# Attention's layer norm for samples 2 to 7 by sums and constant-tile products, in place of transposes both ways

## The reference, cut to what matters

```
def layernorm(x, gamma, beta):
    mu = jnp.mean(x, axis=-1, keepdims=True)
    var = jnp.var(x, axis=-1, keepdims=True)
    return (x - mu) * jax.lax.rsqrt(var + EPS) * gamma + beta
h = layernorm(x, gamma1, beta1)
Q = (h @ Wq + bq) ...
```

## Time and profile before

| what | value |
|---|---|
| median of 3 runs | 1611.33 us (1608.42 to 1615.32) |
| profiled execution, span from first to last instruction | 1610.9 us |
| granted TensorE clock, mean | 0.995 |
| PE busy | 1585.8 us, 98% |
| PEld / DVE / ACT / POOL busy | 1299.5 / 1166.6 / 982.8 / 410.9 us |
| HBM | 125 GB/s over the span |
| a load or store of a whole sample (1024 KB), issue to landing | 4.3 to 5.1 us, median |

### The profile page before, as it was taken

The page is one execution under the profiler, slowest core; times in us unless marked ns, Lnnn a source line. Parts: engine busy times, 40 slices in busy tenths (PEclk is TensorE's granted clock), DMA queues, the critical chain, the costliest instruction groups (busy, mean ns, idle before and its releaser), DMA issues.

```text
span 1610.9 us, 27177 instructions
## 1 busy us (share of the span) xinstructions
PE 1585.8 (98%) x9296; PEld 1299.5 (81%) x9298; DVE 1166.6 (72%) x2767; ACT 982.8 (61%) x2331; POOL 410.9 (26%) x605
## 2 busy tenths in 40 slices
PE   7999999999999999999999999999999999999999
PEld 4688786777777777777777688898999999999998
DVE  7999888786969686868778576785655656565643
ACT  6888766887878787878778755352433324242422
POOL 8998810313222313131312110201010110202010
PEclk8999999999999999999999999999999999999999
DMA  7042135543545444444337435866464555556361
GB/s 308 0 183 97 66 126 126 149 130 92 138 95 139 100 115 122 111 116 115 88 90 214 167 152 207 303 262 232 178 234 170 213 225 188 212 178 265 142 211 68
DMA packets 62257, 254.79 MB, mean 158 GB/s; under 512 B 10628, under 2 KB 16004, under 8 KB 46760
## 3 DMA queue, kind: packets, MB, share of 16 engines
q1 hardware_dynamic: 62120, 253.06, 48.2%
HBM read 153.93 MB, written 48.23 MB: 125 GB/s over the span
## 4 chain that ended last, share of the span: by engine, by line
PE 90%; POOL 3%; DMA 2%; DVE 2%; ACT 1%; issue 1%; SPq 1%; POOLq 0%; DVEq 0%; ACTq 0%
PE psum L83 24%; PE psum L84 23%; PE psum L85 23%; PE psum L1529 5%; PE psum L1549 5%; PE psum L1579 4%; PE psum L1470 1%; DMA k_weights<-w_factors 1%; PE psum L1478 1%; PE psum L2451 1%; DMA k_raw<-in_t_w 1%; POOL k_gs_square L252 1%; POOL k_gs_root L247 1%; ACT psum L1229 1%; POOL k_gs_scaled L256 1%
## 5 line engine op out<-in xcount | busy, mean ns | idle before, releaser
L1229 ACT ACTIVATE psum<-psum,b_mx 128x512 f32<-128x512 f32 (+3 forms) x512 | 258.9, 509 | 63.2 <-DVE b_mx L990 62.0
L990 DVE CUSTOM_DVE_ANT_0 psum<-psum,b_mask 128x512 f32<-128x512 f32 (+3 forms) x512 | 244.7, 506 | 53.0 <-PE psum L1529 48.1
L2398 ACT ACTIVATE k_act<-k_stack_f,k_smalls 128x512 f32<-128x512 f32 x112 | 80.9, 722 | 303.6 <-DVE k_stack_f L2237 297.1
L1241 ACT ACTIVATE k_exps<-psum 128x512 f32<-128x512 f32 (+1 forms) x384 | 194.6, 532 | 59.4 <-PE psum L1549 58.1
L864 POOL TENSOR_SCALAR_AFFINE_SELECT k_exps<-k_exps 128x256 f32<-128x256 f32 x256 | 96.4, 413 | 381.0 <-ACT k_exps L1241 379.1
L2097 POOL TENSOR_SCALAR k_result<-k_result,k_pb 128x512 f32<-128x512 f32 x32 | 59.2, 1866 | 434.9 <-DVE k_result L2156 434.9
L2216 DVE TENSOR_TENSOR k_act_lo<-k_act,k_act_hi 128x512 fp32r<-128x512 f32 x112 | 77.2, 690 | 120.6 <-ACT k_act_hi L2401 120.6
L83 PE MATMUL psum<-k_act_hi,k_w_hi 128*128 128x512 f32 x384 | 150.8, 393 | 0.0
L84 PE MATMUL psum<-k_act_lo,k_w_hi 128*128 128x512 f32 x384 | 150.5, 392 | 0.0
L85 PE MATMUL psum<-k_act_hi,k_w_lo 128*128 128x512 f32 x384 | 150.2, 391 | 0.0
L2237 DVE TENSOR_TENSOR k_raw<-psum,k_raw 128x256 f32<-128x256 f32 x168 | 70.5, 421 | 106.0 <-PE psum L85 95.4
(11 more groups left out here) (372 smaller groups left out, 4418.2 us busy)
## 6 DMA issues: line engine op xcount, KB each, us to landing
k_stack<-w_factors SPq DMA_DIRECT2D x35, 1792.0 KB, 7.7
k_stack<-k_samples SPq DMA_DIRECT2D x384, 128.0 KB, 2.4
k_weights<-w_factors SPq DMA_DIRECT2D x17, 1792.0 KB, 7.5
x<-k_tokens SPq DMA_DIRECT2D x10, 1024.0 KB, 4.3
k_tokens<-x SPq DMA_DIRECT2D x8, 1024.0 KB, 5.1
d<-k_result SPq DMA_DIRECT2D x32, 256.0 KB, 2.9
k_raw<-x SPq DMA_DIRECT2D x8, 1024.0 KB, 4.8
k_raw<-d SPq DMA_DIRECT2D x8, 1024.0 KB, 7.1
```

Of the source, the lines that this page charges most:

```text
L990: last = dve.tensor_tensor_reduce(got, got, mask[:, S - width:S], -INV_SQRT_DH, -2.0 * MASKED, ALU.add, ALU.min, mx[n % 2][:, h, t:t + 1])
L1229: act.activation(sc(n, u)[:, at:at + width], sc(n, u)[:, at:at + width], ACT.Exp, bias=mx[n % 2][:, h, t:t + 1], scale=-1.0, accum_out=sum ...
L1241: act.activation(exps[n % 2][:, h, at:at + width], by_key(n, u)[:, 0:width], ACT.Exp, scale=INV_SQRT_DH).then_inc(k_act, 1)
L2398: act.activation(act_f[:], whole_tile, ACT.Gelu, bias=small(smalls, "b1", 2 * pair % M + second)).then_inc(pair_gelu, 1)
```

## The change

For samples 2 to 7 nothing is turned. POOL adds the four pieces of a sample to one 128x512 tile, splits that sum in a high and a low part (`sample_sum`, five instructions), and PE multiplies both with a constant 128x128 tile of 1/512 (`mean_product`, two matmuls), which leaves the mean of each token on every partition. ACT copies it to SBUF (`mean_copy`), DVE subtracts it from the four pieces (`centre`), ACT squares them (`squares`), POOL sums and splits again (`square_sum`), PE multiplies again (`variance_product`), ACT makes a first reciprocal root by Ln and Exp on 128x512 (`rough_rstd`), DVE does one Newton step in three instructions (`refine`) and multiplies the four pieces (`multiply`), ACT applies gamma and beta from SBUF (`scale_spread`), POOL splits as before (`split_spread`). The 32 transposes, four copies, four scalings out of PSUM, four `statistics`, four `normalise` and one `prepare_rstd` of each such sample go. `BANK_ORDER` loses eight uses and gains two; `values_out(b, 3)` and `values_out(b, 2)` move by a place on DVE. On SP, the load `sample_in(b + 2)` goes from group 1 to the end of group 2. POOL makes two constants in the head. The rest of the diff renumbers semaphores that the samples 0, 1 and the second layer norm now share.

```diff
 (BANK_ORDER)
-     ("tin", 1, 0), ("q", 0, 2), ("k", 0, 2), ("tin", 1, 1), ("tin", 1, 2), ("tin", 1, 3), ("v", 0, 3),
+     ("mean", 1, 0), ("q", 0, 2), ("k", 0, 2), ("v", 0, 3), ("var", 1, 0),
      ("v", 0, 2)),
-    (("tb", 1, 0), ("q", 0, 3), ("k", 0, 3), ("tb", 1, 1), ("tb", 1, 2), ("wo", -1, 0), ("tb", 1, 3), ...
+    (("q", 0, 3), ("k", 0, 3), ("wo", -1, 0), ("wo", -1, 1), ("q", 1, 0), ("k", 1, 0), ...
 (SP, slots)
-                if g == 1 and b + 2 < B:
-                    sample_in(b + 2)
...
                 stack_rows(n + 1, (2, 3))
+                if g == 2 and b + 2 < B:
+                    sample_in(b + 2)
 (POOL)
+        def sample_sum(b):
+            wait_taken(pool, ("st", b, 1))
+            pool.tensor_tensor(tok[:, 0, :], x[:, 0, :], x[:, 1, :], ALU.add).then_inc(mean_sums, 1)
+            for j in (2, 3):
+                wait_taken(pool, ("st", b, j))
+                wait_sums(pool, b, j - 1)
+                pool.tensor_tensor(tok[:, 0, :], tok[:, 0, :], x[:, j, :], ALU.add).then_inc(mean_sums, 1)
+            wait_sums(pool, b, 3)
+            pool.tensor_copy(sums_r[:, 0, :], tok[:, 0, :]).then_inc(mean_sums, 1)
+            wait_sums(pool, b, 4)
+            pool.tensor_tensor(sums_r[:, 1, :], tok[:, 0, :], sums_r[:, 0, :].bitcast(F32), ALU.subtract)...
 (POOL, slots)
                 cut_later(n - 2, 1)
                 if g == 2 and b + 1 < B:
                     for j in range(J):
-                        split(b + 1, j)
+                        split_spread(b + 1, j)
+                if g == 1 and b + 1 < B:
+                    square_sum(b + 1)
                 cut_later(n - 1, 0)
-                if g == 1 and b + 1 < B:
-                    prepare_rstd(b + 1)
+                if g == 0 and b + 1 < B:
+                    sample_sum(b + 1)
 (DVE)
+        def centre(b, j):
+            wait_taken(dve, ("mean", b, 0))
+            dve.tensor_tensor(tok[:, j, :], x[:, j, :], tok[:, J - 1, :], ALU.subtract).then_inc(mean_out, 1)
+        def refine(b, part):
+            bank, y, step = pj(("var", b, 0)), x[:, 3, :], x[:, 0, :]
+            if part == 0:
+                wait_squares(dve, b, J + 2)
+                dve.scalar_tensor_tensor(step, bank, LN_EPS, y, ALU.add, ALU.mult).then_inc(pj_dve, 1)
+            (parts 1 and 2: step = (step * -0.5) * y; step = (step + 1.5) * y)
+        def multiply(b, j):
+            wait_spread(dve, b, J + 2)
+            dve.tensor_tensor(tok[:, j, :], tok[:, j, :], x[:, 0, :], ALU.mult).then_inc(mean_out, 1)
 (DVE, first_steps from max_unit(n + 1, 3) on)
+            max 3, max 4, centre 0, centre 1, max 5, maxima_out(n, 1), centre 2, centre 3, max 6, max 7, ...
+            ... values_out(b, 3), maxima_out(n + 1, 0), max 11, refine 0
 (DVE, last_steps)
+            max 0, values_out(b, 2), shift_rows(n - 1, 1), refine 1, max 1, refine 2, max 2, max 3, multiply 0,
+            max 4, maxima_out(n - 1, 1), multiply 1, max 5 to 7, qk_out, shift_rows, qk_out, multiply 2, max 8,
+            max 9, multiply 3, max 10
 (ACT, first_steps)
+            exps(n+1, 2), by_key(n-1, 11), mean_copy, by_key(n, 0), exps(n+1, 3), exps 4, by_key 1, exps 5,
+            squares 0, 1, 2, log_sums, exps 6, squares 3, exps 7, by_key 2 to 5, ctx_high, by_key 6, exps 8,
+            by_key 7, exps 9, by_key 8, by_key 9, rough_rstd, by_key 10, exps 10
 (ACT, last_steps)
+            exps(n, 0) to (n, 5), scale 0, by_key 0, by_key 1, exps 6, scale 1, by_key 2, log_sums, exps 7,
+            by_key 3, by_key 4, ctx_high, exps 8, scale 2, by_key 5, exps 9, scale 3, by_key 6, ...
 (PE)
+        def mean_product(b):
+            wait_sums(pe, b, 5)
+            out = claim(("mean", b, 0))
+            pe.matmul(out, mean_of[:], sums_r[:, 0, :], start=True, stop=False)
+            pe.matmul(out, mean_of[:], sums_r[:, 1, :], start=False, stop=True).then_inc(pj_full, 1)
 (mean_product stands after qk_piece(b, 2, 1); variance_product, built alike, after score_by_key(n, 9))
```

More of the change, by code:

```diff
@@ L596 @@
 AFTER = B
+SPREAD = range(2, B)
+TURNED_AT = {b: k for k, b in enumerate(b for b in range(B + 1) if b not in SPREAD)}
 U_TILES = ((T - 1,), (T - 2, 0), (1,))
@@ L795, in sample_in @@
             if b:
-                wait_full(sp, ("tin", b - 1, T - 1))
+                if b - 1 in SPREAD:
+                    wait_normalised(sp, b - 1)
+                else:
+                    wait_full(sp, ("tin", b - 1, T - 1))
                 sp.wait_ge(x2_st, 16 * b)
@@ L1116, in first_steps @@
                 max_unit(n + 1, k)
+            shift_rows(n, 1)
+            max_unit(n + 1, 3)
+            max_unit(n + 1, 4)
             if b + 1 < B:
-                statistics(b + 1, 0)
-            shift_rows(n, 1)
-            for k in range(3, 6):
-                max_unit(n + 1, k)
+                centre(b + 1, 0)
+                centre(b + 1, 1)
+            max_unit(n + 1, 5)
             maxima_out(n, 1)
+            if b + 1 < B:
+                centre(b + 1, 2)
+                centre(b + 1, 3)
             max_unit(n + 1, 6)
@@ L1156, in last_steps @@
             qk_out(n + 1, 1)
-            for k in range(8, 11):
-                max_unit(n, k)
+            multiply(b + 1, 2)
+            max_unit(n, 8)
+            max_unit(n, 9)
+            multiply(b + 1, 3)
+            max_unit(n, 10)
             ctx_low(n - 2)
@@ L1259, in scale_back, with mean_copy, squares, rough_rstd @@
                            scale=small(smalls, gamma, j)).then_inc(pj_act, 1)
+        def mean_copy(b):
+            wait_full(act, ("mean", b, 0))
+            act.activation(tok[:, J - 1, :], pj(("mean", b, 0)), ACT.Copy).then_inc(pj_act, 1)
+        def squares(b, j):
+            wait_spread(act, b, j + 1)
+            if j == 0:
+                act.wait_ge(x2_st, 16 * (b + 1))
+            act.activation(x[:, j, :], tok[:, j, :], ACT.Square).then_inc(mean_act, 1)
+        def rough_rstd(b):
+            y = x[:, 3, :]
+            wait_full(act, ("var", b, 0))
+            act.wait_ge(mask_made, 5)
+            wait_sums(act, b, 8)
+            act.activation(y, pj(("var", b, 0)), ACT.Ln, bias=eps[:]).then_inc(mean_act, 1)
+            wait_squares(act, b, J + 1)
+            act.activation(y, y, ACT.Exp, scale=-0.5).then_inc(mean_act, 1)
+        def scale_spread(b, j):
+            wait_normalised(act, b, j + 1)
+            act.activation(tok[:, j, :], tok[:, j, :], ACT.Identity, bias=small(smalls, "beta1", j),
+                           scale=small(smalls, "gamma1", j)).then_inc(mean_act, 1)
         def p_parts(b):
@@ L1354, in last_steps @@
             log_sums(n - 1, 1)
-            scale_back(b + 1, 0)
-            for k in range(6):
-                exponentials(n, k)
+            exponentials(n, 0)
+            exponentials(n, 1)
+            exponentials(n, 2)
+            exponentials(n, 3)
+            exponentials(n, 4)
+            exponentials(n, 5)
+            scale_spread(b + 1, 0)
             exponentials_by_key(n - 1, 0)
@@ L1682, in first_steps @@
             qk_piece(b, 2, 1)
+            if b + 1 < B:
+                mean_product(b + 1)
             score(n + 1, 2)
@@ L2463, in spread @@
         def spread(b):
-            pe.wait_ge(mv_set, T * b)
+            pe.wait_ge(mv_set, before + T * b)
             for t in range(T):
```

165 lines of the change are left out of this document (106 added, 59 removed).

## The result

The changed kernel took 1625.59 us (median of 4 runs, 1623.54 to 1629.66), the kernel before 1610.09 on the same chip (4 runs, 1608.42 to 1615.32). The ratio is 1.0100 with a 95% interval of 1.0085 to 1.0115: slower by one per cent. The forecast was 1614, with a range that ended at 1623. The profiled execution of the changed kernel has a span of 1627.9 us, the longest of its four (the others 1621.8, 1622.6, 1625.2).

The account below looks back on a forecast made before the run. PE, busy 98% of the span, was taken as the bound. Per sample, 2.52 us won against 3.2 of stalls, small gaps allowed for, lost 0.5; six samples gave +3.0, hence 1614 us, range 1598 to 1623.

Parts of the forecast that it names:

- A: Value copy: PE reaches the bank that `q` of group 2 claims before DVE's copy ends; 0.33 us (0.25 to 0.4).
- C: PE's unit by key 4 behind the context waits for ACT's added copy and four squares; 1.14 us (0.6 to 1.6).
- D: In `last_steps`, score unit 4 waits because DVE's value copy and Newton step precede max 1; 0.54 us (0 to 0.9).
- E: In `last_steps`, unit by key 2 waits for DVE's multiplications and an ACT scaling; 0.83 us (0.3 to 1.5).
- rivals 2 and 3: POOL's slow mean delays `mean_product`, 1631 us, chance 0.12; Square or Ln changes ACT's table, about 1628, chance 0.03.
- Rival 1: ACT and DVE keep up with 14 us of slack each; stalls 1.2 us or fewer a sample, 1596 to 1603; chance 0.29.
- Behind the context: Unit 5 waits for exponentials 7 and a scaling, 0.2 us (0 to 0.6), and one more unit 0.1.
- POOL's interference: DVE instructions with two SBUF inputs wait up to 1.3 us behind POOL's; without it E would be about 0.5.

Follow-up runs that it names:

- pool_narrow: Changed kernel with POOL's six additions of a sample on 64 columns instead of 512; 1627.5 us, ratio 1.0093.
- scale_late: Changed kernel with ACT's scaling of piece 0 moved behind units by key 0 and 1 of `last_steps`; 1627.72 us, ratio 1.0097.
- newton_late: Changed kernel with DVE's Newton steps 1 and 2 moved behind maximum units 1 and 2 of `last_steps`; 1624.34 us, ratio 1.0080.
- dve_narrow: Changed kernel with DVE's Newton steps and four multiplications on 8 columns instead of 512; 1618.37 us, ratio 1.0046.
- last_late: Changed kernel reordered in `last_steps`: ACT's scalings and DVE's multiplications and Newton steps later, value copy behind maximum 1; 1622.47 us, ratio 1.0077.
- act_narrow: Changed kernel with ACT's squares 1 to 3 and four scalings on 8 columns instead of 512; 1616.86 us, ratio 1.0038.
- The two reorderings together, all_late: Changed kernel with the order of last_late plus maxima, exponentials and units by key ahead of late centring and squares; 1618.87 us, ratio 1.0051.
- the three after them: Added in turn to all_late: PE's score units 1 and 2 earlier, 1616.08 us; ACT's square 3 later, 1614.39; first scaling behind exponentials 8, 1613.26.
- sq_narrow: Changed kernel with ACT's squares 1, 2 and 3 on 8 columns instead of 512; 1622.51 us, ratio 1.0058.
- both_narrow: Changed kernel with the edits of dve_narrow and act_narrow together; 1612.13 us, ratio 1.0008.
- all_pe_sq: all_late with PE's score units 1 and 2 earlier and ACT's square 3 behind unit by key 4; 1614.39 us, ratio 1.0031.

## Why the prediction was wrong

**What held.** The mechanism: PE saves its 2.5 us a period (3.46 for the groups less 0.92), and all of it goes into waits for ACT and DVE at A, C, D and E, each at the place and with the releaser that was named. The durations: squares 0.62, scalings 0.80, POOL's additions 1.29 and cast 0.61, `centre`, `refine` and `multiply` 0.68 and 0.69, the mean copy 0.60. E came as 0.83 to the hundredth, A as 0.30 against 0.33. POOL was just in time, and no activation table was loaded during attention (rivals 2 and 3 fall; both kernels load four in all, the last two at 246 and 922 us in the changed one). The moved load cost nothing that shows in PE's waits. Rival 1, that 14 us of slack would take the added work, is refuted in its premise: 17 and 19 us of slack did not.

**The step that failed is the sum of the stalls**, 3.2 us a period against 4.0 measured, with the longer steps behind them left out (0.67) and 0.17 taken off. By size:
- C was put at 1.14 and measured 1.50. I walked ACT to unit by key 4 and stopped: "unit 4 comes behind 3, a little more". The units behind waited again, 0.49 in all, because squares and exponentials 7 had pushed a queue of four units together (the row at 517.23 holds four without a gap), and PE takes them two banks at a time.
- D was put at 0.54 and measured 0.79. The walk of DVE was exact (2.7 us from the start of maximum 0 to the end of maximum 1, 527.58 to 530.3), but ACT began at 530.38 and ended at 531.28, and PE went at 531.45: 0.2 to 0.3 us of handing over from engine to engine, which a sum of durations hasn't.
- The restart was left out. The first matmul behind a wait costs 0.10 to 0.12 more: 0.30 for A, D and E. The two products cost 1.29 and not 0.92, 0.37 more: a restart behind the mean's wait, and a wait with restart behind the variance product, for a value copy that the walk did not look at. The earlier trace rows show a step of the same size: behind the transposes the score unit took 0.32 and not 0.23 to its successor, and I counted that as a gain of removing it (0.09 of each group) and looked for no price of adding one. In both cases the traces have the weights loaded only as the matmul starts (501.81 before, 505.46 after); that the cause is one and the same is not shown.
- Behind the context 0.48 came instead of 0.30.
- 0.17 was subtracted because a stall would cover small gaps that PE had anyway. PE idles 0.02 us in the 69 us of the earlier trace rows and 0.15 in the whole period; there was nothing to cover. The end of the period brought another 0.09.

These are 1.67 us a period, ten in all: 1614 would have been 1624. The span of the profiled execution, 1627.9, has 3.0 more for the two half-clock stretches, which no step had, 1.9 behind the last period and 1.0 less in the head. The shortest of the four executions (1621.8, granted clock 0.996 against 0.992) probably had fewer such stretches; that is not shown.

**The half-clock stretches are not mere luck.** The traces of all sixteen kernels have eight of them between 300 and 800 us, where every kernel is in the middle of attention. All eight are in the six kernels in which PE waits 0.89 us or more ahead of unit by key 4 (changed kernel, pool_narrow, scale_late, newton_late, dve_narrow, last_late), and each begins 1.9 to 2.5 us behind that wait. The other ten kernels, the one before among them, wait 0.78 or less ahead of units by key 4 and 6 and have none. So the stalls of the change seem to bring these 3.0 us as well; but 28 waits of the same length have no stretch behind them, nor have those of 1.26 to 1.28 us ahead of the transposed maxima, and what decides is not shown.

**The range was too narrow on this side.** The high ends of the steps added up to 1628, and I gave that 0.06. Nearly all errors had one sign, since each was a cost left out of a walk that adds durations and follows only the first waiter. Where six waits in a row are estimated by the earliest one that binds, the errors don't cancel.

**One number was right by luck, and one size was wrong without harm.** The 0.83 at E was said to need POOL's interference, and 0.5 without it. In the changed kernel no multiplication met a POOL instruction (POOL has nothing between 528.8 and 536.2, and `multiply` 2 at 540.54 began as a subtraction ended), and the stall was 0.83 by durations alone: the agreement to the hundredth is luck. And I put DVE's added work at 2 us; its busy time in a period rose by 0.6 only. That did not help: D and E hang on where the operations stand. The same holds for ACT: dve_narrow and act_narrow show 1.6 and 1.15 us of a period for them, by taking work away at these places.

What stays open: of the 1.9 us behind the last period I know only that they lie in the tail of attention and after it. No run was made to move the half-clock stretches.

## What to carry to other kernels

When one engine is busy 99.8% of a period, work taken off it is worth what the others can still hand over in time at each bank, not what they have idle on average: go through their lists to the *second* and third waiter behind every inserted instruction. Add 0.1 us for each wait that is new, besides its length. Moving the inserted work later carries the stall along to another bank, and can bring two engines side by side that exclude each other: 0.80 us of a period in four of the orders tried here. The two reorderings together gave back 1.3 us of the period (0.6 and 0.7), the three after them 0.15, 0.25 and 0.2.

## What the runs showed of the hardware

- A matmul that waited takes 0.33 or 0.34 us to its successor instead of 0.23 (the projection product behind the value copy, the mean product, the value product behind the variance product), and at D and E 0.10 more than the same matmul of before. At unit by key 4 it took no more than before (0.33 and 0.35).
- TensorE fell to half clock (granted 0.50, the 1.2 GHz level) for 3.4 us at a time, up to four times between 250 and 1600 us of an execution, each worth 1.5 us in this kernel. act_narrow, sq_narrow, both_narrow and all_late show none there, the changed kernel four (260.1, 604.8, 775.5, 826.7), the kernel before two (259.1, 812.1). So two executions of one kernel may differ by 1.5 us for each of them. The eight between 300 and 800 us in all traces each begin 1.9 to 2.5 us behind a PE wait of 0.89 us or more ahead of unit by key 4.
- A DVE product of two SBUF tiles took 1.49 us instead of 0.69 beside a POOL subtraction (all_pe_sq; 24 times in four kernels); POOL's cast behind it took 1.08 instead of 0.61.
